# Decoder layer in one launch: row statistics of the first attention on ScalarE, half of a remainder on GpSimd, another order of transposes

## The reference, cut to what matters

```python
x = _layernorm(x + _L0_attn_ref(x, Wq, Wk, Wv, Wo))            # 32 heads of 16, 8 key heads, causal, rotary
x = _layernorm(x + _L0_xattn_ref(x, ctx, ctx, pos, mask, ...)) # 32 heads of 128, 8 key heads
x = _layernorm(x + _L0_ffn_ref(x, ...))                        # gated by clusters

def _layernorm(x, axis=-1, eps=1e-05):
    m = jnp.mean(x, axis=axis, keepdims=True)
    v = jnp.var(x, axis=axis, keepdims=True)
    return (x - m) / jnp.sqrt(v + eps)
```

## Time and profile before

| | |
|---|---|
| median of 3 runs | 807.41 us (807.27 to 809.64) |
| profiled execution | 806.26 us, span of its instructions 803.0 us |
| TensorE busy | 755.2 us (94%) |
| VectorE busy | 596.4 us (74%) |
| ScalarE busy | 322.0 us (40%) |
| GpSimd busy | 400.6 us (50%) |
| granted TensorE clock, mean | 0.994 of full speed |

### The profile page before, as it was taken

How to read it: one execution, slowest core, us unless ns; L and a number is a source line. 1 busy time by engine, 2 the same in 40 slices (tenths; PEclk the granted TensorE clock), 3 DMA queues, 4 the chain that set the end, 5 groups by cost and what they waited for, 6 DMA issues and landing times.

```text
span 803.0 us, 13860 instructions
## 1 busy us (share of the span) xinstructions
PE 755.2 (94%) x4800; PEld 646.9 (81%) x4800; DVE 596.4 (74%) x1143; ACT 322.0 (40%) x684; POOL 400.6 (50%) x381
## 2 busy tenths in 40 slices
PE   4689999979999999999999999999999999999996
PEld 3677777769878887888888888888888888888875
DVE  4778888887877676777667667766776777688777
ACT  3545555563333333242333333233333323234335
POOL 7566666674544464444446445444544534445303
PEclk9899999999999999999999999999999999999999
DMA  9700004012263222422322342232233222141002
GB/s 232 156 18 18 16 16 121 3 26 84 54 158 80 53 55 64 103 69 52 78 52 52 73 107 55 52 78 52 55 77 103 52 53 79 27 101 31 1 1 104
DMA packets 107873, 53.52 MB, mean 67 GB/s; under 512 B 80448, under 2 KB 96960, under 8 KB 107840
## 3 DMA queue, kind: packets, MB, share of 16 engines
q1 hardware_dynamic: 107008, 51.51, 25.9%
q10 hardware_dynamic: 576, 1.05, 0.4%
q0 software_dynamic: 256, 0.52, 0.2%
HBM read 32.62 MB, written 2.10 MB: 43 GB/s over the span
## 4 chain that ended last, share of the span: by engine, by line
PE 67%; DVE 16%; issue 5%; POOL 5%; DMA 2%; ACT 2%; SPq 2%; DVEq 0%; POOLq 0%; ACTq 0%
PE bank L730 18%; PE bank L665 16%; PE bank L491 10%; DVE arena_r L1588 5%; PE s_bank L744 4%; PE bank L541 3%; PE s_bank L746 2%; PE bank L565 2%; PE bank L714 2%; DVE small L1676 2%; PE bank L885 2%; DVE arena_f L1670 1%; PE s_bank L714 1%; DMA arena_f<-in_L_attn_Wo 1%; PE s_bank L565 1%
## 5 line engine op out<-in xcount | busy, mean ns | idle before, releaser
L994 ACT ACTIVATE arena_r<-bank 128x256 fp32r<-128x256 f32 (+2 forms) x249 | 105.1, 459 | 215.7 <-PE bank L697 83.8
L730 PE MATMUL bank<-arena_r 128*128 128x512 f32 x768 | 191.4, 398 | 0.0
L665 PE MATMUL bank<-arena_r 128*128 128x512 f32 x720 | 185.2, 400 | 2.1 <-POOL arena_r L1431 1.6
L730 PEld LDWEIGHTS bank<-arena_r 128*128 128x128 f32 x768 | 139.6, 188 | 26.9
L665 PEld LDWEIGHTS bank<-arena_r 128*128 128x128 f32 x720 | 130.6, 188 | 31.4 <-POOL arena_r L1431 2.0
L491 PE MATMUL bank<-arena_r 128*128 128x256 f32 (+1 forms) x1056 | 146.7, 294 | 2.2 <-DVE arena_r L1588 1.4
L491 PEld LDWEIGHTS bank<-arena_r 128*128 128x128 f32 x1056 | 137.3, 191 | 9.4 <-DVE arena_r L1588 2.0
L1588 DVE TENSOR_TENSOR arena_r<-bank,arena_r 128x256 fp32r<-128x256 f32 (+2 forms) x217 | 99.7, 485 | 56.9 <-ACT arena_r L994 56.6
L994 ACT ACTIVATE arena_r<-arena_f 128x512 fp32r<-128x512 f32 (+2 forms) x178 | 104.5, 637 | 61.9 <-DMA arena_f<-arena_f 46.7
L1588 DVE TENSOR_TENSOR arena_r<-arena_f,arena_r 128x512 fp32r<-128x512 f32 (+1 forms) x95 | 87.2, 926 | 19.7 <-ACT arena_r L994 19.7
L1422 POOL TENSOR_TENSOR arena_f<-arena_f 128x512 f32<-128x512 f32 x30 | 39.1, 1304 | 114.5 <-DVE arena_f L1757 114.4
(11 more groups left out here) (164 smaller groups left out, 1175.8 us busy)
## 6 DMA issues: line engine op xcount, KB each, us to landing
arena_f<-arena_f SPq DMA_DIRECT2D x120, 128.0 KB, 2.5
arena_f<-in_L_xattn_Wo SPq DMA_DIRECT2D x8, 1024.0 KB, 5.9
arena_f<-in_L_xattn_Wq SPq DMA_DIRECT2D x14, 512.0 KB, 4.2
arena_f<-in_x SPq DMA_DIRECT2D x8, 256.0 KB, 2.9
arena_f<-in_x SPq DMA_DIRECT2D x1, 2048.0 KB, 17.9
arena_f<-in_L_xattn_Wk SPq DMA_DIRECT2D x8, 256.0 KB, 3.0
arena_f<-in_L_xattn_Wv SPq DMA_DIRECT2D x8, 256.0 KB, 3.3
arena_f<-in_ctx SPq DMA_DIRECT2D x8, 256.0 KB, 3.5
```

What stands on the lines that cost most here:

```text
L665: mm = pe.matmul(BQ2[f][:], w2q_s[a][:, e, j, f, :], xT[b][:, e, tok], start=(e == 0 and n == 0), stop=(e == EC - 1 and n == 2))
L730: mm = pe.matmul(BO2[i][:], at2[a][:, h, i * P:(i + 1) * P], w2o_s[b][:, h, :], start=(h == 0 and n == 0), stop=(h == HG - 1 and n == 2))
L994: act.activation(dst, src, ACT.Copy).then_inc(done, 1)
```

## The change

For tiles 0 to 5 the row sum, the centred sum of squares and the normalisation of the first layer norm go from VectorE to ScalarE, and the small operations on them to GpSimd; tiles 6 and 7 keep VectorE's. The remainder of the queries is halved: heads 0 to 15 stay on VectorE, heads 16 to 31 go to GpSimd, which signals it on `s_kl` ahead of the keys' (so `s_kl` counts two a tile). In `qk_stage` three query groups come first, then keys, a query group, and keys; the first scores wait for four evictions in place of three. TensorE turns the tokens of w (`x1_stage`) at the end of the step, behind `wo_stage`; ScalarE's copy to `res` and `x1_high` move behind exponential 2, VectorE's `x1_low` behind `masked_max` 3, and `kv_stage` waits for `total(v, 2)`.

```diff
@@ -173,6 +173,7 @@
         sums = small[:, 144:152]
         ndmax = small[:, 208:216]
         cid = small[0:NC, 241:242]
+        sum1, nmean1, var1, shift1 = (small[:, 152 + n:153 + n] for n in range(4))
         tot8, nmean = small[:, 224:232], small[:, 232:240]
         st6b = small[:, 216:222]
         neg2 = small[:, 240:241]
@@ -551,9 +552,11 @@
                 pe.wait_ge(s_ql, t + 1)
                 if tile_stages(t)[2]:
                     pe.wait_ge(s_res, t - 1)
-                for j, (kind, n) in enumerate((("q", 0), ("q", 1), ("k", 0), ("q", 2), ("q", 3), ("k", 1))):
+                for j, (kind, n) in enumerate((("q", 0), ("q", 1), ("q", 2), ("k", 0), ("q", 3), ("k", 1))):
                     if j == 2:
-                        pe.wait_ge(s_kl, t + 1)
+                        pe.wait_ge(s_kl, 2 * t + 1)
+                    if j == 3:
+                        pe.wait_ge(s_kl, 2 * t + 2)
                     if j >= 3:
                         pe.wait_ge(s_qke, 6 * t + j - 2)
                     elif j > 0 and not first:
@@ -578,7 +581,7 @@
 
             def s_stage(t, units, first):
                 even, odd = units
-                pe.wait_ge(s_qke, 6 * t + 3 + 3 * (even // 2))
+                pe.wait_ge(s_qke, 6 * t + 4 + 2 * (even // 2))
                 if even >= 2 or not first:
                     pe.wait_ge(s_cp, 4 * t + odd - 1)
                 for i in range(4):
@@ -620,7 +623,7 @@
                     pt_stage(v, 0)
                     pt_stage(v, 1)
                 if old:
-                    pe.wait_ge(s_cp, 4 * i)
+                    pe.wait_ge(s_rc, 4 * i - 1)
                 kv_stage(i, start)
                 if old:
                     pt_stage(v, 2)
@@ -633,13 +636,13 @@
                 if old:
                     pv_stage(v, 0, not oldest)
                     pv_stage(v, 1, not oldest)
-                if oldest:
-                    x1_stage(w, i)
                 if start:
                     table_turn()
                 s_stage(i, (2, 3), start)
                 if old:
                     wo_stage(v, i, not oldest)
+                if oldest:
+                    x1_stage(w, i)
 
 
             BQ2, BKV2, TR2, BS2, BO2 = banks[0:2], banks[2], banks[3], banks[4:6], banks[6:8]
@@ -825,6 +828,7 @@
             pe.wait_ge(s_rk, T)
             pe.wait_ge(s_vr, T)
             pe.wait_ge(c_xl, 2)
+            pe.wait_ge(s_x1l, T - 2)
             kv_proj(0, 0)
             kv_proj(0, 1).then_inc(c_kv, 1)
             x1_stage(v - 1, None, banks[7])
@@ -1027,6 +1031,25 @@
                     act.wait_ge(s_wo, v)
                 copy(at1[0], banks[7][:].rearrange("p (b a q) -> p a b q", b=2, a=4), s_ah)
 
+            def residual(w):
+                return res[:, bass.ds(w, 1), :].rearrange("p t n -> p (t n)")
+
+            def tile_sum1(w):
+                act.wait_ge(s_res, w + 1)
+                act.sem_inc(s_gate, 1)
+                act.activation(x1n, residual(w), ACT.Identity, accum_out=sum1).then_inc(s_ln, 1)
+
+            def tile_squares1(w):
+                act.wait_ge(s_ln, 4 * w + 2)
+                act.sem_inc(s_gate, 1)
+                act.activation(x1n, residual(w), ACT.Square, bias=nmean1, scale=1.0,
+                               accum_out=var1).then_inc(s_ln, 1)
+
+            def norm1(w):
+                act.wait_ge(s_x1c, 2 * w + 1)
+                act.sem_inc(s_gate, 1)
+                act.activation(x1n, residual(w), ACT.Identity, bias=shift1, scale=rstd).then_inc(s_x1n, 1)
+
             def expo(v, u):
                 act.wait_ge(s_sub, 4 * v + u + 1)
                 act.activation(p1[u], p1[u], ACT.Exp, scale=SCALE1).then_inc(s_ex, 1)
@@ -1059,7 +1082,7 @@
                 n_q = n_k = 0
                 if old:
                     act.wait_ge(s_s, 4 * i)
-                for j, kind in enumerate("qqkqqk"):
+                for j, kind in enumerate("qqqkqk"):
                     act.wait_ge(s_qk, 6 * i + j + 1)
                     if j == 3 and following:
                         x_high(i + 1)
@@ -1074,9 +1097,14 @@
                 if not following:
                     wq_high(0, 2)
                     wq_high(0, 3)
+                if oldest:
+                    tile_sum1(w)
+                    tile_squares1(w)
                 if old:
                     at_high(v, not oldest)
                 expo(i, 0)
+                if oldest:
+                    norm1(w)
                 if not old:
                     table_copy(0)
                     table_copy(1)
@@ -1085,14 +1113,13 @@
                 if old:
                     act.wait_ge(s_pv, i)
                 copy(v_blocks(vpad[0]), v_st, s_vh)
-                if oldest:
-                    act.wait_ge(s_x1n, w + 1)
-                    copy(res[:, bass.ds(w, 1), :].rearrange("p t n -> p (t n)"), x1n, s_x1c)
-                    x1_high(w)
                 if not following:
                     wkv_high(0, 0)
                     wkv_high(0, 1)
                 expo(i, 2)
+                if oldest:
+                    copy(residual(w), x1n, s_x1c)
+                    x1_high(w)
                 expo(i, 3)
 
             def x1_high(w, bank=banks[2]):
@@ -1374,8 +1401,22 @@
                 pool.tensor_tensor(cut(p1[u], b=8, k=S), cut(p1[u], b=8, k=S), bcast(sm1[u], 2, S),
                                    ALU.mult).then_inc(s_pn, 1)
 
+            def mean1(w):
+                pool.wait_ge(s_ln, 4 * w + 1)
+                pool.sem_inc(s_gate, 1)
+                pool.tensor_scalar(nmean1, sum1, -1.0 / E, None, ALU.mult).then_inc(s_ln, 1)
+
+            def moments1(w):
+                pool.wait_ge(s_ln, 4 * w + 3)
+                pool.sem_inc(s_gate, 1)
+                pool.tensor_scalar(var1, var1, 1.0 / E, EPS, ALU.mult, ALU.add).then_inc(s_ln, 1)
+                pool.wait_ge(s_ln, 4 * w + 4)
+                pool.tensor_tensor(rstd, var1, half, ALU.pow).then_inc(s_lp, 1)
+                pool.wait_ge(s_lp, w + 1)
+                pool.tensor_tensor(shift1, nmean1, rstd, ALU.mult).then_inc(s_x1c, 1)
+
             def root1(w):
-                pool.wait_ge(s_ln, 3 * w + 3)
+                pool.wait_ge(s_ln, 3 * w + T + 1)
                 pool.tensor_tensor(rstd, mv[:, 1:2], half, ALU.pow).then_inc(s_lp, 1)
 
             def tile_steps(i):
@@ -1389,6 +1430,10 @@
                     norm(v, 3)
                 pool.wait_ge(s_rk, i + 1)
                 pool.tensor_tensor(t1k, t1k, t2k, ALU.add).then_inc(s_ks, 1)
+                pool.wait_ge(s_qh, i + 1)
+                sq = stack_q.rearrange("p h (a b d) -> p h a b d", a=2, b=2)[:, H1 // 2:]
+                pool.tensor_tensor(sq[:, :, 1], bcast(t1q.rearrange("p (h d) -> p h d", h=H1)[:, H1 // 2:], 2, 2),
+                                   f32(sq[:, :, 0]), ALU.subtract).then_inc(s_kl, 1)
                 pool.wait_ge(s_kh, i + 1)
                 sk = stack_k.rearrange("p g (a b d) -> p g a b d", a=4, b=2)
                 pool.tensor_tensor(sk[:, :, :, 1], bcast(t1k.rearrange("p (g d) -> p g d", g=G1), 2, 4),
@@ -1397,8 +1442,10 @@
                     wq_low(0, 0)
                     wq_low(0, 1)
                 if oldest:
-                    root1(w)
+                    mean1(w)
                 sub(i, 0, not old)
+                if oldest:
+                    moments1(w)
                 sub(i, 1, not old)
                 norm(i, 0)
                 pool.wait_ge(s_vh, i + 1)
@@ -1602,6 +1649,7 @@
                 dve.wait_ge(s_q, t + 1)
                 if not first:
                     dve.wait_ge(s_ql, t)
+                    dve.wait_ge(s_kl, 2 * t)
                 dve.tensor_tensor(t1, q, bcast(rope1[:, 0:D1], 1, H1), ALU.mult)
                 sin = bcast(rope1[:, D1:D1 + 8], 1, H1)
                 dve.scalar_tensor_tensor(t2[:, :, 0:D1:2], q[:, :, 1:D1:2], -1.0, sin, ALU.mult, ALU.mult)
@@ -1612,7 +1660,7 @@
                 t1, t2 = (v.rearrange("p (h d) -> p h d", h=G1) for v in (t1k, t2k))
                 dve.wait_ge(s_kv, t + 1)
                 if not first:
-                    dve.wait_ge(s_kl, t)
+                    dve.wait_ge(s_kl, 2 * t)
                 dve.tensor_tensor(t1, k, bcast(rope1[:, 0:D1], 1, G1), ALU.mult)
                 sin = bcast(rope1[:, D1:D1 + 8], 1, G1)
                 dve.scalar_tensor_tensor(t2[:, :, 0:D1:2], k[:, :, 1:D1:2], -1.0, sin, ALU.mult, ALU.mult)
@@ -1626,8 +1674,8 @@
 
             def q_low(t):
                 dve.wait_ge(s_qh, t + 1)
-                sq = stack_q.rearrange("p h (a b d) -> p h a b d", a=2, b=2)
-                low(sq[:, :, 1], bcast(t1q.rearrange("p (h d) -> p h d", h=H1), 2, 2), sq[:, :, 0], s_ql)
+                sq = stack_q.rearrange("p h (a b d) -> p h a b d", a=2, b=2)[:, 0:H1 // 2]
+                low(sq[:, :, 1], bcast(t1q.rearrange("p (h d) -> p h d", h=H1)[:, 0:H1 // 2], 2, 2), sq[:, :, 0], s_ql)
 
             def at_low(v):
                 dve.wait_ge(s_ah, v + 1)
@@ -1641,15 +1689,17 @@
```

(18 more changed lines are left out.)

## The result

The kernel with the change takes 820.58 us (median of 4 runs, 819.90 to 823.41), the kernel before 807.34 us beside it (4 runs, 806.66 to 809.64). The ratio is 1.0165, 95% interval 1.0141 to 1.0189: 13.2 us slower, where 6.8 was forecast (814.2, with a range of 809 to 820). The profiled execution took 820.98 us, its span is 819.0.

What follows compares the result with a forecast made beforehand. A circle of waits through four engines, not VectorE's queue, was taken as the bound. Losses of 0.3 (tiles 0, 1), 1.0 (tile 2), 5.2 (tiles 3 to 6) and 0.3 (tile 7) made 6.8 us: 814.2, range 809 to 820.

Steps and rivals of the forecast that it cites:

- the first scores: In `qk_stage`, scores wait for the key group in fourth place: start 9.3 us behind `rope_q` against 8.80, 0.5 later.
- VectorE's side of the end of the circle: `x1_low`, now VectorE's last instruction, and `total(v, 2)` delay `rope_q` to 21.6 us, 0.25 later than TensorE's route.
- the tiles that pay in full: First attention: tiles 3 to 6 lose 1.3 us each, 5.2 together; tile 2 loses 1.0.
- The circle through four engines: First attention's middle tiles: a chain of waits through VectorE, TensorE, GpSimd and ScalarE sets the 20.32 us period.
- rival 3: VectorE's queue was the bound: 1.9 us off each of six tiles, 11.4 us faster, 796 us; chance 0.08.
- rival 2: Losses hidden, both GpSimd instructions at 1.27 us; only turned tokens cost, 0.5 a tile: 807.4 to 810 us; chance 0.10.
- rival 1: GpSimd's half of `q_low` goes first, VectorE's stands 1.27 us: period 22.2, 817 to 819 us; chance 0.10.
- One sign of being wrong: Forecast wrong if GpSimd's half of `q_low` ends before 5.7 us behind `rope_q`; then the scores move up.
- the bare turning: `x1_stage` behind `wo_stage` no longer fills TensorE's idle time: 0.52 us a tile on the circle.
- The statistics: First layer norm's sum, squares and normalisation on ScalarE, moments on GpSimd: taken to cost nothing.
- Exactly at the edge: GpSimd's moments, 1.5 us before `sub(i, 1)`, just fit: nothing taken, between nothing and 0.3 us a tile.
- rival 4: GpSimd's moments cost more than assumed: 0.3 us a tile, 2 us, 816 us; counted inside the forecast's own case.

Runs made afterwards that it cites:

- l: Kernel before with only the order of transposed groups changed (three query groups, keys fourth, scores waiting for four evictions): 809.06 us, ratio 1.0033, period 20.67 us.
- b: Changed kernel with the whole query remainder `q_low` back on VectorE, group order and norm part kept: 814.11 us, ratio 1.0092 to the kernel before, period 21.65 us.
- e: Kernel before with only the tokens turned last, behind the output projection; statistics and normalisation stay on VectorE: 811.75 us, ratio 1.0060, period 21.31 us.
- c: Kernel before with the norm part alone (statistics on ScalarE and GpSimd, tokens turned last), query part unchanged: 812.05 us, ratio 1.0072, period 21.31 us.
- a: Changed kernel with GpSimd's half of the query remainder waiting until VectorE's half is done: 816.51 us, ratio 1.0131 to the kernel before, period 22.25 us.
- h: Changed kernel with ScalarE's `x_high` one place later, behind the key group's eviction: 816.94 us, ratio 1.0111 to the kernel before, period 21.99 us.
- d: Kernel before with the query part alone (half the remainder on GpSimd, three query groups ahead of keys), norm part as before: 817.71 us, ratio 1.0136.
- g: Kernel before with `q_low` in two halves, both on VectorE, the second behind `p_low` 2 and 3: 805.41 us, ratio 0.9974; repeated, 805.54 us, 0.9981.

## Why the prediction went wrong in size

What failed is two terms of the sum and a count: the first scores (+0.5 us a tile taken, +1.0 measured), VectorE's side of the end of the circle (0.25 later than TensorE's taken, 0.77 measured), and the tiles that pay in full (four and a part taken, five measured). Which of the two halves of `q_low` goes first was taken wrongly too, but that is worth only 0.15 a tile. The median also holds some 2.7 us outside these tiles, where the prediction had 0.3.

**The mechanism held.** The circle through four engines, not VectorE's queue, sets the period. Taking work off VectorE gave nothing (rival 3 is out), the losses were not hidden (nor rival 2), and the kernel lost where two of its steps were put on the circle: the first scores, and `x1_low` ahead of `rope_q`. The parts measured alone add up:

| part | from | us a tile |
|---|---|---|
| order of groups | l | +0.35 |
| half of `q_low` on GpSimd, on top of it | after less b | +0.75 |
| tokens turned last | e | +0.99 |
| statistics moved | c less e | 0 |
| sum | | +2.09 |
| measured | after | +2.08 |

The forecast was 1.3 a tile. Step by step:

**The first scores: +0.5 forecast, +1.0 measured.** This is the first mis-sized term. The walk let VectorE's half go first and be over at R+5.0, and found the keys last at R+7.5. In the trace GpSimd was first by 0.02 us, the halves began at R+4.32 and R+4.34, and VectorE's ended at R+6.14: rival 1, which had 0.10. Rival 1 gave a period of 22.2 and 817 to 819 us. It came nearer than the forecast, but not because of who was first: with VectorE first (a) the period is 22.25. So its closeness is luck. Its queries at R+6.9 are a slip as well: by its own terms, 4.34 + 1.27 + 0.68, they are R+6.3, and they came at R+6.20. One sign of being wrong was named and did appear, GpSimd's half over before R+5.7 (R+5.60), but the scores did not move up for it: the keys stood behind it and ended at R+7.28. With VectorE first `k_low` ended at R+7.63 and not R+7.5, TensorE took the fourth group at R+7.75 and not R+7.55, and from there to the scores it was 1.9 us where I had 1.75. So even with the order that I took, the term is 0.86 (R+9.66). Three small steps (0.13, 0.07, 0.16) were each taken at too little; the other 0.15 of the measured 1.0 go with GpSimd being first. The prices of the instructions were right: GpSimd's 1.27 was 1.28 or 1.29, VectorE's 0.68 was 0.68.

**Where the order weighs.** I had counted `x_high`'s 0.5 ahead of the key eviction. Experiment h, which puts it behind, gives 0.41 back, and l shows 0.35 for the order with `q_low` untouched. This part was sized about right.

**The end of the circle: VectorE's side later than TensorE's by 0.25 forecast, 0.77 measured.** I had `x1_low` 5.98 behind `at_low` and `rope_q` 7.48 behind it. They came 6.19 and 7.77 behind it in the changed kernel, 6.20 and 7.69 in c. The parts up to `x1_high` were right (`sub(i, 2)` at 3.30 behind `at_low`, as foretold); the handover from ScalarE to `x1_low` (0.17) and a tenth from there to `rope_q` were left out. GpSimd's `sub(i, 2)` and ScalarE's `x1_high`, which ends at 147.64, in the changed kernel:

```profile
144.92 1.05 POOL L1396 TENSOR_TENSOR arena_f<-arena_f,small 128x512 f32<-128x512 f32 x1
```

```profile
147.06 0.58 ACT L998 ACTIVATE arena_r<-bank 128x512 f32 x1
```

This second mis-sized term is 0.3 a tile. On the other side `x1_stage` cost TensorE 0.35 and not 0.52, hidden behind it: the bare turning is not what is paid, `x1_low` is. 0.5 + 0.3 is all of 2.08 - 1.3.

**The statistics: nothing, right.** (The instructions taken off VectorE add up to 1.56 us and not to the 1.7 of the prediction; with the 0.53 they are its 2.1. No term of the sum hangs on it.) GpSimd's moments took 1.09 (140.90 to 141.99) and not 1.5, ScalarE had 1.2 us to spare, and c and e have the same period. "Exactly at the edge" did not become a cost, and rival 4 is out.

**The count of tiles.** I gave tile 2 only 1.0 and four tiles 1.3. The period that begins with tile 2's `rope_q` holds tile 2's late `x1_low` already, and lost 2.09: five full tiles, 10.3 us in the two profiled executions. Tile 7 (0.3 forecast), from its `rope_q` to the last turned probabilities (the earlier trace rows has them in the kernel before), took 19.96 us in the second executions against 19.83. In the first pair it took 21.57 against 19.82; there the transposes of `qk_stage` ran in part at half clock.

**Together.** 10.4 for five tiles and 0.1 for tile 7 stand against 5.2 + 1.0 + 0.3 of the forecast. With 2.08 in each of five tiles, and the 0.3 for tiles 0 and 1, it would have been 807.4 + 10.4 + 0.1 + 0.3 = 818.2.

**What stays open.** The medians differ by 13.2, so some 2.7 us lie outside these tiles. In the first profiled pair what lies outside is 3.5 us in tile 0 (26.55 us from its `rope_q` to the next, 23.09 before), 1.75 in tile 7 and 1.4 behind it, less 1.0 at the start. The changed kernel's execution had more half clock there: 17.0 us against 6.8 ahead of tile 2, and 3.4 against none both in tile 7 and at about 750 us. But tile 0 took 25.05 and 25.87 in the second pair, with the sign turned round. Kernel d has the same sort of excess, 12.0 against 5.6; the others have -0.6 to 1.8 us. The mean granted clock of the single timed executions says part of it. Of d's four, two had 0.982 (819.63 and 818.59 us) and one 0.989 (814.26). Beside them the kernel before took 810.3 at 0.982 and 805.7 at 0.988. So at an equal clock d is 8.3 to 9.3 us slower, and about half of its excess goes with the lower clock. Three of the changed kernel's four executions had 0.984 or 0.985, with a median of 820.2. The kernel before, in its four executions at 0.983 to 0.986 beside e, g and h, had a median of 810.5, and the 9.7 us between the two are no more than the five periods give. The fourth had 0.988 and took 823.41, which this doesn't explain. Whether the half on GpSimd brings stretches of half clock on more often was not settled: they come and go between executions of the same kernel.

## What to carry to other kernels

Before moving work off the busiest engine, walk once round the circle that sets the period and see whether the freed instructions lie on it; here 2 us less on an engine that was busy 18 of 20.3 us brought nothing, while two steps put on the circle cost 2.1. A step that waits for two engines is as late as the later of them, so halving an instruction over two engines helps only if the second engine has nothing else due for the same step: halving it in time on its own engine was the better cut (0.26 us less a tile, against 0.75 more). When a loss is summed along a chain of handovers, add each handover at its measured gap (0.07 to 0.2 us here) and not at nothing: five such steps, each taken too short, were some 0.6 of the 0.78 us by which a tile was misjudged.

## What the runs showed of the hardware

- *GpSimd against VectorE with two SBUF inputs.* The one that stands does so for the rest of the other's instruction and ends a fixed time behind it. Where the two are due 0.01 or 0.02 us apart, the rows don't tell who will stand. In the changed kernel GpSimd's half starts that much ahead, and VectorE's stood in tiles 2 to 6 of both executions. But in tile 7 of the second, with the same lead by the rows, it was GpSimd's that stood, in 1.84 us, and VectorE's ran in 0.69 (the two rows below). VectorE's 0.68 ended 0.54 behind GpSimd's (131.32 + 1.28 = 132.60; 133.14) and took 1.80. GpSimd's `k_low`, issued at 132.55, ended 1.14 behind VectorE's (134.28) and took 1.73; against the whole `q_low` it ended 1.13 behind (123.78; 124.91). In g VectorE's second half met the last 0.22 us of `k_low` and took 0.77, ending 0.55 behind it. So the price of a meeting is what is left of the other instruction, less some 0.13 us. The Trainium skill (SBUF — State Buffer, Summary: rules for kernel authors) says that the second to issue fully blocks until the first is done; the trace agrees, and here two engines blocked each other one after the other.

```profile
175.10 1.84 POOL L1435 TENSOR_TENSOR arena_r<-arena_f,arena_r 128x512 fp32r<-128x512 f32 x1
```

```profile
175.11 0.69 DVE L1635 TENSOR_TENSOR arena_r<-arena_f,arena_r 128x512 fp32r<-128x512 f32 x1
```

- *The clock at half speed comes and goes.* In the same kernel, the same 6.8 us stretch ran at a mean granted clock of 0.66 and of 1.00 of full speed (full is 2.4 GHz, the half 1.2). In the kernel before, TensorE's product of 12 in `b_stage` of tile 1 took 5.49 us in one such stretch and 3.03 at full clock. That is enough to turn round the sign of a difference in the first tiles, and periods in the middle tell more than spans.
- *Row statistics on ScalarE* took 0.65 us for the sum and 0.72 for the squares of 512 values, and the read of the accumulator behind each 0.2.
